# Latent attention on one core: products with the latents split by row halves into two PSUM banks, a pair's scores in one bank, the third pair's queries behind the first scores

## The reference, cut to what matters

```python
    q_c = _rmsnorm(x @ wq_down, q_norm_w)
    q_nope = (q_c @ wq_up) ...; q_rope = _apply_rope(q_c @ wq_rope)
    kv_c = _rmsnorm(x @ wkv_down, kv_norm_w)
    k_nope, v = parts of kv_c @ wkv_up; k_rope = _apply_rope(x @ wk_rope)
    scores = (q_nope . k_nope + q_rope . k_rope) / sqrt(192), causal within each of the 16 sequences of 32 rows
    out = softmax(scores) @ v, heads side by side; return out @ wo
```

## Time and profile before

| what | value |
|---|---|
| median of 3 runs | 711.43 us (709.33 to 711.96) |
| the profiled execution | 711.55 us |
| its span, first to last instruction | 709.8 us |
| mean granted TensorE clock | 0.991 |
| TensorE, weight loads, VectorE, ScalarE busy | 96%, 63%, 61%, 39% |
| DMA, mean over the span | 59 GB/s |
| attention with latents, first queries to last rows out | 600.8 to 677.2 us of the span |

### The profile page before, as it was taken

The page is one execution under the profiler, slowest core; times in us unless marked ns, Lnnn a source line. Parts: engine busy times, 40 slices in busy tenths (PEclk is TensorE's granted clock), DMA queues, the critical chain, the costliest instruction groups (busy, mean ns, idle before and its releaser), DMA issues.

```text
span 709.8 us, 20893 instructions
## 1 busy us (share of the span) xinstructions
PE 678.3 (96%) x9196; PEld 445.3 (63%) x9196; DVE 429.7 (61%) x998; ACT 273.7 (39%) x502; POOL 65.9 (9%) x132
## 2 busy tenths in 40 slices
PE   9999999999997999999999999999999899999976
PEld 5666666556654666777777566667666665366754
DVE  4444456567484655555553863545968765677777
ACT  3444444444342423334334744444334454011124
POOL 1100001001001011111111003010202002000000
PEclk9999999999999999999999999999999999889999
DMA  6161111015001601000003510211294000000000
GB/s 226 60 173 47 31 31 60 32 32 181 31 2 60 240 31 31 32 31 30 2 1 96 203 59 31 62 32 38 65 277 102 3 4 0 3 2 3 3 0 31
DMA packets 42330, 42.20 MB, mean 59 GB/s; under 512 B 15872, under 2 KB 33024, under 8 KB 41984
## 3 DMA queue, kind: packets, MB, share of 16 engines
q1 hardware_dynamic: 42240, 40.86, 18.8%
HBM read 40.33 MB, written 0.52 MB: 58 GB/s over the span
## 4 chain that ended last, share of the span: by engine, by line
PE 81%; DVE 12%; ACT 3%; issue 2%; SPq 1%; DMA 1%; POOL 0%; DVEq 0%; ACTq 0%
PE psum L385 14%; PE psum L377 14%; PE psum L1115 7%; PE psum L448 5%; PE psum L399 5%; PE psum L426 4%; PE psum L413 4%; PE psum L1162 4%; PE psum L1121 3%; PE psum L1824 2%; PE psum L1801 2%; PE psum L1146 2%; PE psum L1844 2%; PE psum L1135 1%; PE psum L1805 1%
## 5 line engine op out<-in xcount | busy, mean ns | idle before, releaser
L377 PE MATMUL psum<-arena 128*128 128x512 f32 x256 | 123.0, 606 | 2.1 <-DMA arena<-in_ctxT 2.1
L385 PE MATMUL psum<-arena 128*128 128x256 f32 x512 | 123.3, 385 | 0.2 <-ACT arena L649 0.2
L385 PEld LDWEIGHTS psum<-arena 128*128 128x128 f32 x512 | 93.4, 190 | 22.2 <-issue 9.7
L675 ACT ACTIVATE arena<-arena 128x512 f32<-128x512 f32 x64 | 48.6, 806 | 73.0 <-DVE arena L802 73.0
L377 PEld LDWEIGHTS psum<-arena 128*128 128x128 f32 x256 | 44.4, 189 | 44.9 <-issue 42.7
L448 PEld LDWEIGHTS psum<-arena 128*17 128x17 f32 x4096 | 39.3, 96 | 38.9 <-issue 32.1
L669 ACT ACTIVATE arena<-psum,arena 128x512 f32<-128x512 f32 x64 | 42.4, 687 | 39.3 <-DVE arena L789 39.1
L802 DVE TENSOR_SCALAR arena<-psum 128x512 f32<-128x512 f32 x64 | 40.9, 685 | 26.1 <-PE psum L413 22.9
L448 PE MATMUL psum<-arena 128*17 128x32 f32 x4096 | 49.1, 195 | 4.1 <-DVE arena L794 1.3
L1115 PE MATMUL psum<-y_cols,arena 128*128 128x512 f32 x112 | 52.2, 599 | 0.0
L789 DVE TENSOR_REDUCE arena<-psum 128x1 f32<-128x512 f32 x64 | 42.4, 685 | 16.1 <-PE psum L399 15.9
(11 more groups left out here) (248 smaller groups left out, 971.1 us busy)
## 6 DMA issues: line engine op xcount, KB each, us to landing
arena<-in_ctxT SPq DMA_DIRECT2D x32, 512.0 KB, 3.8
arena<-in_L_attn_Wv SPq DMA_DIRECT2D x1, 2048.0 KB, 8.3
arena<-in_L_attn_Wq SPq DMA_DIRECT2D x8, 256.0 KB, 2.9
arena<-in_L_attn_Wk SPq DMA_DIRECT2D x8, 256.0 KB, 3.3
arena<-in_L_attn_Wo SPq DMA_DIRECT2D x1, 2048.0 KB, 12.3
arena<-in_L_ffn_w_gating SPq DMA_DIRECT2D x1, 2048.0 KB, 7.6
arena<-in_L_attn_wo SPq DMA_DIRECT2D x1, 2048.0 KB, 12.4
arena<-in_wq_upT SPq DMA_DIRECT2D x1, 1536.0 KB, 7.9
```

The source lines that it names most:

```text
L377: last = nc.tensor.matmul(bank, wkv[:, c, i * P:(i + 1) * P], x[:, c, :], start=(c == 0), stop=(c == NC - 1))
L385: last = nc.tensor.matmul(bank[:, kk * D:(kk + 1) * D], x[:, c, k * P:(k + 1) * P], wkv[:, c, D:2 * D], start=(c == 0), stop=(c == NC - 1))
L675: nc.scalar.activation(pTk[b % 2][k], clip[k // 2][:, k % 2, :], ACT.Exp, bias=mb[:, b, k:k + 1], scale=m01[:, b, k:k + 1]).then_inc(s_exp, 1)
```

## The change

The products with the latents are cut by row halves: each half of `pT` (now 64 columns wide) holds only its own two sequences, its product goes over 64 rows and 64 columns, and half r writes bank 2 + r. The scores of both heads of a pair lie in bank 4, opened by one mask product of 256 columns over the first 64 rows. `scores(0)` holds no `queries`; the three steps of `queries(2)` follow it. The copy reads two banks and writes `oT` in the old order.

```diff
-    pT = [late([P, 2, NT, P]) for _ in range(2)]
+    pT = [late([P, 2, NT, 2 * SQ]) for _ in range(2)]
...
+    OB = e.psum[:, 2:4, 0:2 * P]
+    SC = B[4][:, 0:2 * NT * SQ].rearrange("p (c t k) -> p c t k", c=2, t=NT)
...
-        for c in range(2):
-            nc.tensor.matmul(B[3 + c][:, 0:NT * SQ], identm[half(c), 0, :], identm[half(c), 1, :], start=True, stop=False)
+        nc.tensor.matmul(B[4][:, 0:2 * NT * SQ], identm[half(0), 0, :],
+                         identm[half(0), 1, :].unsqueeze(1).to_broadcast([64, 2, NT * SQ]), start=True, stop=False)
         for t in range(NT):
-            if t and j + 2 < PAIRS:
+            if t and 0 < j < PAIRS - 2:
                 queries(pe, j + 2, t - 1)
-            elif t % 2:
+            elif t % 2 and j:
                 out_rows(pe, j - 2, t // 2)
...
-                        last = nc.tensor.matmul(B[3 + c][k * SQ:(k + 1) * SQ, t * SQ:(t + 1) * SQ],
+                        last = nc.tensor.matmul(SC[k * SQ:(k + 1) * SQ, c, t, :],
...
         last.then_inc(s_scores, 1)
+        if j == 0:
+            for i in range(3):
+                queries(pe, 2, i)
...
         for t in range(NT):
             for c in range(2):
-                last = nc.tensor.matmul(OB[half(c), t * P:(t + 1) * P], krow[:, t, 0:KR], pT[u][:, c, t, :],
-                                        start=True, stop=True)
+                for r in range(2):
+                    last = nc.tensor.matmul(OB[half(c), r, t * 64:(t + 1) * 64], krow[half(r), t, 0:KR], pT[u][half(r), c, t, :],
+                                            start=True, stop=True)
...
-        nc.scalar.activation(oT[j % 2], OB, ACT.Identity, scale=vvec).then_inc(s_oT, 1)
+        nc.scalar.activation(oT[j % 2].rearrange("p (t r x) -> p r t x", r=2, x=64),
+                             OB.rearrange("p r (t x) -> p r t x", x=64), ACT.Identity, scale=vvec).then_inc(s_oT, 1)
...
-            a = 32 * k
-            nc.vector.transpose(pT[u][a:a + 32].rearrange("p c t k -> p (c t) k")[:, :, a:a + 32],
+            a, q = 32 * k, 32 * (k % 2)
+            nc.vector.transpose(pT[u][a:a + 32].rearrange("p c t k -> p (c t) k")[:, :, q:q + 32],
                                 flat(pr[a:a + 32])).then_inc(s_pT, 1)
```

More of the change, by code:

```diff
@@ L1691, in mla @@
     pr, mx, sm = late([P, 2, NT, SQ]), late([P, 2, NT]), late([P, 2, NT])
-    pT = [late([P, 2, NT, P]) for _ in range(2)]
+    pT = [late([P, 2, NT, 2 * SQ]) for _ in range(2)]
     B = e.B
-    FOLD, DOWN, QB, OB, ACC = (B[0], B[1]), (B[2], B[3], B[4], B[5]), (B[0], B[1], B[5]), B[2], (B[6], B[7])
+    FOLD, DOWN, QB, ACC = (B[0], B[1]), (B[2], B[3], B[4], B[5]), (B[0], B[1], B[5]), (B[6], B[7])
     HEAD, LAST = (0, 1, 2), (NT - 1,)
@@ L1698, in mla @@
            [B[i][:, a * P:(a + 1) * P] for i, a in ((5, 0), (0, 0), (5, 1), (0, 1))])
-    SC = e.psum[:, 3:5, 0:NT * SQ].rearrange("p c (t k) -> p c t k", t=NT)
+    OB = e.psum[:, 2:4, 0:2 * P]
+    SC = B[4][:, 0:2 * NT * SQ].rearrange("p (c t k) -> p c t k", c=2, t=NT)
     N_W, N_HEADS = 13, 7
@@ L1823, in scores @@
                         r = slice(t * P + k * SQ, t * P + (k + 1) * SQ)
-                        last = nc.tensor.matmul(B[3 + c][k * SQ:(k + 1) * SQ, t * SQ:(t + 1) * SQ],
+                        last = nc.tensor.matmul(SC[k * SQ:(k + 1) * SQ, c, t, :],
                                                 (both, turned)[i][u][c][rows, r], kT[rows, i, r],
-                                                start=False, stop=(i == 1 and t == NT - 1))
+                                                start=False, stop=(i == 1 and t == NT - 1 and c == 1))
         last.then_inc(s_scores, 1)
+        if j == 0:
+            for i in range(3):
+                queries(pe, 2, i)
     def values(pe, j):
```

## The result

Seven executions of each: 707.51 us median (707.09 to 712.41) against 711.58 us (709.33 to 713.56), ratio 0.9953 with a 95% interval of 0.9931 to 0.9974. The forecast of 704.4 us asked for 7.1 us less; 4.1 us came between the medians, 3.3 us by the ratio. The time lies in the range given, but the gain is about half of what was forecast, and its interval ends well short of 7.1 us.

What follows compares the result with a forecast made beforehand. TensorE was taken to set the pace, with a gap and a clock fall in the fifth stage. 4.25 us from the clock and 2.85 from the rest made 7.10: 711.55 - 7.10 = 704.4 us, range 702.9 to 708.9.

Steps and rivals of the forecast that it cites:

- The chain of steps: Fifth stage, followed from scores(0) through the pairs to values(7): starts and waits forecast in turn, 7.10 us less in all.
- Gap: Fifth stage, before scores(1): TensorE's idle 1.18 us would vanish, scores(1) starting at 612.81, not 614.01.
- values: Products with the latents, fifth stage: row halves would take 0.61 us in place of 1.02, saving 0.41.
- the idling before scores(2): TensorE after values(0) would idle 0.94 us, waiting for VectorE's maximum and subtraction of pair 1.
- queries(2) without score blocks between its steps: Three query steps of pair 2 behind scores(0): 3.17 us, from 609.64 to 612.81.
- the clock's term: Fifth stage: half-clock fall after the gap, priced at 3.51 + 0.74 = 4.25 us, would be gone.
- the rest: The forecast saving apart from the clock's term: 2.85 of 7.10 us.
- Rival (b): Values does not quicken, staying at 1.02 us: 706.9 us (706.6 by the 25 ns floor); chance 0.09.
- rival (c): Values slower: 64 x 64 tiles do not overlap, 2.72 us per values, 719.8 us in all; chance 0.05.
- rival (a): The clock falls all the same, one fall of the same price: 708.7 us; chance 0.12.
- The row set against rival (a): Evidence against a new fall: an earlier window, TensorE busy only 1.39 of 3.00 us, kept the clock at 1.00.
- Sum: 6.28 + 0.82 = 7.10 us: Fifth stage: 6.28 us ahead at values(6), plus 0.41 there and 0.41 with values(7).

Runs made afterwards that it cites:

- r1_before: Unchanged copy of the kernel before, timed and profiled again: 712.99 us median, ratio 1.0016 to before, stage 72.73 us.
- r1_after: Unchanged copy of the changed kernel, timed and profiled again: 708.27 us median, ratio 0.9940 to the kernel before, stage 69.84 us.
- r3_after_again: The changed kernel a third time, unchanged: 707.27 us median, ratio 0.9953 to the kernel before, stage 69.54 us.
- the first set: Both kernels again and each part of the change alone, timed in the same rounds: kernel before 712.99 us, changed kernel 708.27 us.
- the three sets: Timed follow-ups against the kernel before: copies and parts alone; fills and a moved rotation; smaller fills. Medians 705.58 to 712.99 us.
- r1_only_halves: Changed kernel with queries of pair 2 put back in scores(0); row halves, one score bank, one mask product kept: 709.37 us, 0.9973 to before.
- r3_after_both: Changed kernel with rotation (2, 0) later and six and seven filling products at two earlier idle places: 706.65 us, ratio 0.9946 to before.
- r2_after_filled: Changed kernel with twelve filling products at each of two idle places, first and fourth stage code: 712.40 us, ratio 1.0007 to before.
- r2_after_both: Changed kernel with twelve filling products at each of two earlier idle places and rotation (2, 0) later: 710.72 us, ratio 0.9996 to before.
- r2_after_rotate: Changed kernel with VectorE's rotation (2, 0) moved behind the product of softmax(0): 706.73 us, ratio 0.9939 to before.

## Why the prediction was right and wrong

**The chain of steps held.** Gap closed; values 0.62 us (0.61 forecast); mask 0.21 (0.20); the idling before scores(2) 1.00 (0.94), ended by VectorE's subtraction; scores(2) 18.86 us behind the first queries (19.02); period 8.02 (7.99); scores(7) 1.17 behind values(5), no gain there; the whole stage 7.14 us less than the same stage of the profiled execution before (7.10). One term was oversized: queries(2) without score blocks between its steps took 612.51 to 615.39, 2.88 us and not 3.17, so scores(1) came 1.50 us earlier in the stage and not 1.20. VectorE's wait took about half of this back. The split of the sum was less good than the sum: the clock's term was 0.28 us too large and the rest 0.32 too small.

**Rival (b)** did not come. The 32 instructions of 64 x 64 tiles started within 0.62 us, 19 ns each with the change of tile kind counted in. By the rule of the Trainium skill (TensorE: Matmul & The Clock Gate, Part 1), that starts never come closer than about 25 ns, values would have stayed near 0.97 us; this trace disagrees. Nor did rival (c), nor rival (a) in its own terms: no profile of the changed kernel has a fall in the stage.

**The step that failed** is the 4.25 us of the clock, in "Sum: 6.28 + 0.82 = 7.10 us, of which 4.25 are the clock's". As a term of the profiled execution it was nearly right (3.97; scores(2) would have waited 0.20 us for the subtraction at full clock as well, seen at 625.68 in r1_before). As a term of the kernel's time it was wrong: it stood in one of six profiles. That the profiled execution lay 0.12 us from the median seemed to make it typical. It was not: it had one fall of 10.2 us in the stage and none elsewhere, while others of nearly the same time had one or two of 3.4 us in the second and fourth stage, and started the changed stage at 603.2 to 605.8 us in place of 600.8. Those falls come in the changed kernel too: r1_after has two and the profile after one, r3_after_again none. Of 95 later executions of the kernel before, eight show a mean granted clock under 0.991, and they took 714.6 to 715.6 us; none shows 0.991. I asked of the fall what caused it, but not how often it comes, though three times that differ by 2.6 us were shown.

The row set against rival (a) was such a single event too. The earlier trace rows is the place in the second stage at which many other profiles fell, and this execution idled there for only 1.14 us:

```profile
229.04 0.44 PE L158 MATMUL psum<-ident,y_rows 128*128 128x128 f32 x2 [1.14 <-DVE y_rows L142]
```

Thirteen of the seventeen other profiles idle there for 1.74 us, and nine of them fell.

What is left of the sum without the clock, 2.85 us, is the forecast's own figure for the rest; the runs show 72.73 - 69.55 = 3.2. The measured differences are 3.0 to 4.1 us between medians of one set, and the same code timed twice in the first set gave 711.96 and 712.99 us. Part of what stands above 3.2 is the clock: over the executions of the three sets the mean granted clock is 0.9951 before (95 executions, mean 711.87 us), and with those of the result it is 0.9959 after (26, mean 707.80). Executions with the same mean clock can be compared: at 0.997 the medians are 710.00 (17 before) and 707.00 (7 after), at 0.994 711.99 (6) and 708.61 (9), at 0.998 710.29 (8) and 706.95 (3): 3.0, 3.4 and 3.3 us. A line fitted through all of them, with one slope for both kernels, gives 0.65 us for each 0.001 of clock and 3.5 us (plus or minus 0.3) between the kernels. So of the 4.1 us between the means about 0.6 are the clock's and 3.2 the stage's. The other 0.3 us stay open and aren't clear of the scatter; the waits on "issue", which move from kernel to kernel, and the DMAs at the start are candidates that no run here separated.

Whether the 1.18 us gap brings the fall is only half settled. Two of seven against none of eleven fits; r1_only_halves shows a fall beginning behind it; but five profiles with the gap kept the clock, and filling it in the kernel before brought no time.

## What to carry to other kernels

Before a single event of a profile, such as a clock fall, enters the sum, ask whether it belongs to the kernel or to that execution: take a second profile, or look for the same price in the spread of the times; a total near the median doesn't show it, since another execution pays it elsewhere. Take the sum with and without it, and let the one that leaves it out be the forecast while only one profile shows it. Splitting products into four tiles of half the rows and half the columns paid here (1.02 to 0.62 us for values), but only where what waits behind them was not itself waiting for another engine; whether it needs the two banks was not tried.

## What the runs showed of the hardware

- Four 64 x 64 tiles with 64 moving columns run side by side: 0.62 us for 32 instructions, against 1.02 us for 16 instructions of 128 x 64 with 128 columns. In the trace after, the starts come in groups of four, 7 ns apart, one group every 58 ns (the first is followed after 107); before, in pairs, one pair about every 109 ns behind the first.
- Ahead of the last two us of the span the granted clock fell for 3.4 us in 14 of 18 profiles, 21 times in all, and once for 10.2 us. Nineteen of the 21 short falls came at three places, in the second and the fourth stage, behind idle times of TensorE of 1.74 to 3.05 us. The same place falls in one execution and not in the next: nine of thirteen times behind 1.74 us, and once each not behind 2.13 and 2.55 us.
- TensorE can stand on "issue" in a dense stream of products, where the profile names nothing that it waits for: 0.76 us behind 104 of 128 in r3_after_both, 2.16 us in r2_after_filled and r2_after_both. The place is not the same in every kernel: r2_after_rotate runs the same fifth stage as r3_after_both without this wait. So a filled kernel may lose by it what it gains in the clock.
